# Weight halves made during the second layers and kept in DRAM, constants and bias behind the first inputs, and the first output column group freed before the exponent

## The reference

```
for e in (real, imaginary):                        # first and second layers
    h_e = gelu(layernorm(x @ W1_e.T + b1_e) * g_e + be_e)   # x: 1024 x 2048, W1: 2048 x 2048
    s_e = (h_e @ W2_e.T + b2_e)                             # W2: 2048 x 2048, cut into 4 states of 512
q, k, v for e: s_e @ Wq_e.T + bq_e, ...                     # six 512 x 512 matrices, 8 heads
mag = sqrt(|q . conj(k)|^2 + 1e-8) / 8;  w = softmax(mag)   # over the 4 states
attn_e = (w @ v_e) @ Wo_e.T + bo_e                          # two 512 x 512 matrices
R, I = attn turned by int_Wr[n], int_Wi[n]                  # per state n, eight 512 x 512 matrices
f = cos(phase between states i and j) * strength
sup = normalised sum over i, j of f * (R, I)
amp = |meas (Mr, Mi) applied to sup|;  z = gelu(layernorm(amp @ post_W.T + b))
y = relu(relu([z, x] @ W_top1 + b) @ W_top2 + b) @ W_top3
```

## Time and profile before

| what | us |
|---|---|
| median of 3 runs | 3175.93 |
| lowest, highest | 3175.32, 3177.78 |
| time of the profiled execution | 3182.69 |
| its span | 3181.0 |
| PE busy in it | 2999.9 |
| DVE busy | 1573.5 |
| ACT busy | 1111.3 |

### The profile page before, as it was taken

One profiled execution on the slowest core, in us unless ns is written; L12 is line 12 of the kernel. 1 busy time (PEld: TensorE's weight loads), 2 busy tenths in 40 slices (PEclk: granted clock), 3 DMA queues, 4 the chain that ended last, 5 costly groups with the idle time before them and its releaser, 6 DMA issues. The chain is left out here.

```text
span 3181.0 us, 43948 instructions
## 1 busy us (share of the span) xinstructions
PE 2999.9 (94%) x15808; PEld 2577.4 (81%) x15808; DVE 1573.5 (49%) x2819; ACT 1111.3 (35%) x1873; POOL 232.9 (7%) x241
## 2 busy tenths in 40 slices
PE   7999999999699999999969999999999989999798
PEld 6888888888588877888859999999999977777686
DVE  3222222112531125212156766767757768999973
ACT  3111111111331114211145555555545564555553
POOL 1000000000110011111000000000000000112000
PEclk9999999999899999999989999999999999999899
DMA  5222222121442334332252232232232274444410
GB/s 196 73 76 73 73 75 73 57 65 63 149 143 75 99 96 136 106 99 84 71 185 54 56 90 66 66 86 59 66 92 53 80 189 89 99 88 96 142 41 11
DMA packets 364352, 285.48 MB, mean 90 GB/s; under 512 B 280192, under 2 KB 280320, under 8 KB 364160
## 3 DMA queue, kind: packets, MB, share of 16 engines
q1 hardware_dynamic: 341632, 206.97, 24.3%
q0 software_dynamic: 22656, 77.67, 7.1%
HBM read 194.40 MB, written 90.18 MB: 89 GB/s over the span
## 5 line engine op out<-in xcount | busy, mean ns | idle before, releaser
L50 PE MATMUL banks<-a_whi,a_xhi 128*128 128x512 f32 x1152 | 450.4, 391 | 24.1 <-DVE a_wlo L179 17.6
L51 PE MATMUL banks<-a_wlo,a_xhi 128*128 128x512 f32 x1152 | 449.4, 390 | 0.0
L52 PE MATMUL banks<-a_whi,a_xlo 128*128 128x512 f32 x1152 | 449.3, 390 | 0.0
L50 PE MATMUL banks<-b_ghi,b_whi 128*128 128x512 f32 x1024 | 402.1, 393 | 10.2 <-DVE b_slo L389 8.6
L52 PE MATMUL banks<-b_ghi,b_wlo 128*128 128x512 f32 x1024 | 399.1, 390 | 0.0
L51 PE MATMUL banks<-b_glo,b_whi 128*128 128x512 f32 x1024 | 399.0, 390 | 0.0
L179 DVE TENSOR_TENSOR a_wlo<-a_wraw,a_whi 128x512 fp32r<-128x512 f32 x144 | 99.7, 693 | 577.6 <-ACT a_whi L165 577.6
L165 ACT ACTIVATE a_whi<-a_wraw 128x512 fp32r<-128x512 f32 x144 | 90.9, 631 | 668.1 <-PE banks L52 629.3
L50 PE MATMUL banks<-t_sx,s_whi 128*128 128x256 f32 x1024 | 292.8, 286 | 28.6 <-DVE s_wlo L1267 24.5
L374 DVE TENSOR_TENSOR b_wlo<-b_wraw,b_whi 128x512 fp32r<-128x512 f32 x128 | 88.3, 691 | 444.8 <-ACT b_whi L326 444.6
L52 PE MATMUL banks<-t_sx,s_wlo 128*128 128x256 f32 x1024 | 289.9, 283 | 0.0
(11 more groups left out here) (156 smaller groups left out, 5562.9 us busy)
## 6 DMA issues: line engine op xcount, KB each, us to landing
a_wraw<-w_first SPq DMA_DIRECT2D x144, 256.0 KB, 2.6
b_wraw<-w_second SPq DMA_DIRECT2D x128, 256.0 KB, 2.6
t_sx<-s_scr SPq DMA_DIRECT2D x64, 512.0 KB, 4.5
a_scr<-t_at SPq DMA_DIRECT2D x256, 128.0 KB, 2.1
s_axng<-a_scr SPq DMA_DIRECT2D x64, 512.0 KB, 5.6
s_wraw<-w_pieces SPq DMA_DIRECT2D x82, 256.0 KB, 4.7
h_scr<-a_hst POOLq DMA_DIRECT2D x72, 256.0 KB, 2.7
b_hl<-h_scr POOLq DMA_DIRECT2D x16, 1024.0 KB, 6.0
```

What stands on the lines that cost most here:

```text
L50: mm(out, ahi, bhi, start=first, stop=False)
L51: mm(out, ahi, blo, start=False, stop=False)
L52: return mm(out, alo, bhi, start=False, stop=last)
```

## The change

1. `phase_constants` is gone. POOL makes the constants in the first stage after its 16 loads of the input; SP loads the first nine weight tiles, then the columns and the bias, then goes on.
2. Halves of the late weights are made in the second layers. In chunks 1 to 6 of both branches, 6 pieces each (`PRE`), 4 in the last chunk of the first branch, 6 in the first of the second: SP loads a piece (256 KB), ACT and DVE split it (`pre_high`, `pre_low`, after the ring's own steps j = 3 to 7, by `AFTER`), SP stores both halves (512 KB) to the new `w_scr` in DRAM.
3. `g.hi` and `g.lo` (32 tiles each) now lie where `xhi`/`xlo`, `ghi`/`glo` and `whi`/`wlo` of the stages lay. `load_pieces(q, group)` loads four pieces, high and low, with two transfers of 1 MB. As steps q = 0 to 7 of the last second-layer chunk end, the first 8 groups are loaded over `ghi`, `glo`. The rest follows in the states stage, in place of `piece` on SP. PE waits for the loads (`g.w_in[q]`), and all `pieces` are gone from ACT and DVE.
4. In `block_body`, group 0 of `t_high` and `t_low` comes before `exponent` and `total`.

```diff
@@ first layers @@
+            def load_w(c, k):
+                sp.wait_ge(w_split, c * KI + (k + 1))
+                sp.dma_start(wraw[:, k % RAW, :], g.w_first[c, k]).then_inc(w_loaded[k % RAW], 16)
+            for k in range(KI):
+                load_w(0, k)
+                if k == KI // 2:
+                    sp.dma_start(g.cols[:, :], g.cols_in).then_inc(cols_in, 16)
+                    sp.dma_start(bias[:, :], g.row1.rearrange("c n -> (c n)").partition_broadcast(P)).then_inc(bias_in, 16)
...
@@ second layers @@
+        praw = s.sb("praw", [P, 2, W])
+        pnew = s.sb("pnew", [P, 2, 2, W], F32R)
...
+        AFTER = {3: (0, 1), 4: (2,), 5: (3,), 6: (4,), 7: (5,)}
...
+            def pre_load(p, x):
+                sp.wait_ge(p_split, p + 1)
+                sp.dma_start(praw[:, x % 2, :], g.w_pieces[p]).then_inc(p_loaded[x % 2], 16)
+            def pre_store(p, x):
+                sp.wait_ge(p_split, p + 3)
+                sp.dma_start(g.w_scr[bass.ds(p, 1)].rearrange("o p h w -> p (o h) w"),
+                             pnew[:, x % 2, :, :].bitcast(F32)).then_inc(p_stored[x % 2], 16)
+            def chunk(br, c, n):
                 for j in range(ST):
+                    ring(br * CH + c, j)
+                    if j < min(n, 2):
+                        pre_load(prepared(br, c, j), j)
+                    for x in AFTER.get(j - 1, ()) + ((5,) if j == ST - 1 else ()):
+                        if x < n:
+                            pre_store(prepared(br, c, x), x)
+                        if x + 2 < n:
+                            pre_load(prepared(br, c, x + 2), x + 2)
...
+            for q in range(ST):
+                sp.wait_ge(w_used, (2 * CH - 1) * ST + (SPL + q + 1))
+                g.load_pieces(sp, q, q)
...
+            def pre_high(p, x):
+                act.wait_ge(p_loaded[x % 2], (p - x) * 8 + (16 * (x // 2) + 16))
+                act.wait_ge(p_stored[x % 2], (p - x) * 8 + (16 * (x // 2) + 16))
+                act.activation(pnew[:, x % 2, 0, :], praw[:, x % 2, :], ACT.Copy).then_inc(p_hi, 1)
...
@@ states, SP @@
             sp.wait_ge(projected, LAST_B * 8 + 8)
-            for i in range(NP, NP + 2 * KD):
-                piece(i)
+            for q in range(4):
+                g.load_pieces(sp, q, 8 + q)
             sp.wait_ge(v_full, LAST_B * 4 + 4)
             load(0, 0)
+            for q in range(4, 6):
+                g.load_pieces(sp, q, 8 + q)
             store_a(LAST_B - 1)
             load(0, 1)
-            for i in range(NP + 2 * KD, NP + 4 * KD):
-                piece(i)
             store_a(LAST_B)
...
+            for q in range(6, 8):
+                g.load_pieces(sp, q, 8 + q)
             load(0, 2)
...
+            sp.wait_ge(multiplied, LAST * 8 + 2)
+            g.load_pieces(sp, 0, 16)
+            g.load_pieces(sp, 1, 17)
             load(LAST, 3)
             store(LAST - 2)
+            sp.wait_ge(multiplied, LAST * 8 + 4)
+            g.load_pieces(sp, 2, 18)
+            g.load_pieces(sp, 3, 19)
             sp.wait_ge(multiplied, LAST * 8 + 6)
             sup_back(0)
...
@@ states, ACT (DVE alike, with t_low before total) @@
                 t_magnitude(b)
+                if not first and not last(b):
+                    t_high(b - 1, 0)
                 exponent(b)
                 if not first and not last(b):
-                    for m in range(KD):
+                    for m in range(1, KD):
                         t_high(b - 1, m)
...
@@ build @@
+        def load_pieces(eng, q, group):
+            n = min(KD, NPIECE - group * KD)
+            for h, to in enumerate((g.hi, g.lo)):
+                eng.dma_start(to[:, q * KD:q * KD + n, :].bitcast(F32),
+                              g.w_scr[group * KD:group * KD + n, :, h, :].rearrange("i p w -> p i w")).then_inc(g.w_in[q], 16)
```

More of the change, by code:

```diff
@@ L423, in _ @@
                                           ALU.subtract).then_inc(g_split, 1)
+                    for x in AFTER.get(j, ()):
+                        if x < extra(br, 0):
+                            pre_low(prepared(br, 0, x), x)
                 for j in range(AHEAD):
@@ L429, in _ @@
                         w_low(br * CH + c, j)
+                        for x in AFTER[j]:
+                            pre_low(prepared(br, c, x), x)
                     for j in range(AHEAD):
@@ L436, in _ @@
                     w_low(br * CH + (CH - 1), j)
+                    for x in AFTER[j]:
+                        if x < extra(br, CH - 1):
+                            pre_low(prepared(br, CH - 1, x), x)
                 s_low(br, CH - 1)
@@ L514, in phase_states @@
     with s.ctx:
[L515 to L519 removed]
+        whi, wlo = g.hi, g.lo
         ids = s.sb("ids", [P, TT, N], mybir.dt.int32)
@@ L830, in _ @@
             sup_back(2)
-            for i in range(2 * NP + 4 * KD, 2 * NP + N_TOP):
-                piece(i)
             store(LAST - 1)
@@ L950, in block_body @@
                         o_high(b - 1, m - 1)
-                    if first and m == 1:
-                        pieces(M_V * KD, M_O * KD)
-                    if first and m == 3:
-                        pieces(M_O * KD, NP)
                 if not first:
@@ L1286, in block_body @@
                 shift(b)
+                if not first and not last(b):
+                    t_low(b - 1, 0)
                 total(b)
@@ L1289, in block_body @@
                 if not first and not last(b):
-                    for m in range(KD):
+                    for m in range(1, KD):
                         t_low(b - 1, m)
-            pieces(0, M_V * KD)
             blocks(dve, block_body)
@@ L1513, in _ @@
             tile.units()
-            pieces(2 * NP, 2 * NP + 2 * KD)
             sup_low(0)
@@ L1712, in vectors @@
                             w = (2 * n + (x if part == 0 else 1 - x)) * KD + k
-                            if part == 0 and first:
-                                pe.wait_ge(w_split, NP + w + 1)
+                            if part == 0 and first and k == 0:
+                                pe.wait_ge(g.w_in[2 * n + x], 64)
                             a = ax[:, n % 2, :, k, :]
```

187 lines of the change are left out of this document (80 added, 107 removed).

## The result

The changed kernel takes **3192.84 us** (median of 5 runs, 3190.35 to 3197.01) against 3175.93 us before (3175.15 to 3180.23, 5 runs): a ratio of 1.0051, 95% interval 1.0037 to 1.0065. It is slower, by 16.9 us, where 3150 (3132 to 3170) was predicted: 43 us off. The profiled execution has a span of 3195.3 us, 14.3 more than before.

The account below looks back on a forecast made before the run. PE was taken as the bound nearly everywhere, DVE in the tile loop; terms -8.9 - 6.0 - 14.6 + 13.0 - 1.4 - 8.2 = -26.1 gave 3156.6 us for the profiled execution, 3149.8 by the median, taken as 3150, range 3132 to 3170.

Parts of the forecast that it names:

- the reserve that it gave SP's ring: Second layers: ring loads go out about two steps later, still one or two steps (5.4 us each) before ACT needs them.
- Second layers: Piece splits, 3.7 us per chunk on ACT and DVE each, are covered by PE's matmuls: 0, at worst +3.
- Into the first block: Between second layers and first block, loaded halves replace piece splits, so PE starts at 1615, not 1621.05: -6.0 us.
- Blocks: In fourteen blocks, group 0 ahead of exponent and total ends PE's waits of 1.045 us on average: -14.6 us.
- the margin of 0.2 to 0.3 us: In the blocks, t_low of group 1 ends 0.2 to 0.3 us before PE wants its bank; missing it gives -7.
- End of the blocks: Last block: SP's loads delay the a_scr store, ACT's group 2 comes 16.1 us later, less 3.1 behind it: +13.0 us.
- The first rival: End of the blocks: stores are not held up, giving -3.1 instead of +13.0, so 3134 us; chance 0.13.
- First tile: In the first tile, PE's wait for a negation behind pieces on ACT goes: -1.4 us.
- Pipeline: DVE splits ahead of the first measuring operand (-4.8) and of the first amplitude and its successor (-3.3) go: -8.2 us.
- Start: Until the first matmul: POOL loads x earlier (-3.8) and it lands faster without the bias (-5.2): -8.9 us.
- The second rival: Wait back at blocks' group 3 (+7.6) or chunks losing time behind SP's stores (+13); about 3165, up to 3173; chance 0.2.
- the third: load_pieces moves fewer GB/s than plain pieces, delaying the first block and end of blocks; at 250 GB/s, 3197 us; chance 0.08.

Follow-up runs that it names:

- e1: The changed kernel with 64 bytes per partition allocated ahead of hi and 64 behind lo, so both begin at a multiple of 128: 3163.46 us, ratio 0.9957.
- e2: The kernel before with the first layers' xhi and xlo moved by 64 bytes and all behind them by 128: 3185.7 us, ratio 1.0026.
- e5: The kernel before with the first layers' stationary tiles at sixteen byte offsets, one per step, weights staying at multiples of 128: 3192.97 us (one run).
- e6: The kernel before with 64 bytes allocated ahead of xhi, moving stationary and moving tiles of the first layers together: 3180.07 us (one run).
- e11: The changed kernel with 192 bytes allocated ahead of hi and 64 behind lo, and POOL instead of SP moving the second layers' pieces: 3149.9 us, ratio 0.9911.
- e4: The kernel before with only output group 0 of t_high and t_low put ahead of exponent and total: 3160.42 us, ratio 0.9938.
- e8: e1 with SP's order in the last block changed, 7.3 MB instead of 13.6 MB ahead of the first store: 3160.33 us, ratio 0.9948.
- e7: e1 with the second layers' pieces loaded and stored by POOL instead of SP: 3160.41 us, ratio 0.9945.

## Why the prediction was wrong

Its premise failed, in the first paragraph: "a change that touches no matmul can only win PE's idle time". The change touches no matmul, and it moved an operand of 6528 of them in the first two stages. The pace of PE was taken as fixed, and that is the step that failed: 22.8 + 6.8 = 29.6 us have no term in the sum. The second step that failed is the reserve that it gave SP's ring.

- **First layers: no term; +22.8 us.** The prediction has no line on the new places of `xhi` and `xlo`. e1, e2, e5 and e6 show the cause: the stationary tile lies 64 bytes off the moving one, modulo 256.
- **Second layers: 0, at worst +3; +18.1** (the stretch's 14.7 and the 3.4 won at its end). 6.8 us are the same effect, and 6.1 more stand in the first chunk of the second branch. The prediction named that place and the mechanism (SP "in order behind stores that wait for `pre_low`"), and then gave the ring two steps of reserve. It had none there: ACT waited 6.08 and 5.20 us. The worst case, +3, had no row behind it. A further 3.6 us are lost in the next chunk, where the 5.40 us of idle time were followed by the lower clock, and 1.5 in the first chunk of all, whose first step also ran at a lower granted clock (0.81 over 862.3 to 871.1); what lowered it there, no run took apart. e11, with the places right and SP's ring alone, takes 779.5 us for the whole stretch (before: 782.7) and has none of this.
- **Into the first block: -6.0; -3.4** (24.39 to 20.94). `load_pieces` had the rate assumed. What was late next were the states, as said, and later than said: SP's first load of them, behind the barrier, is at 1646.14, some 15 us after the last second-layer matmul (before: some 9), with the DMA engines full until then.
- **Blocks: -14.6; -17.2 by e4.** The mechanism is right, and the margin of 0.2 to 0.3 us held. A wait of 1.05 us ended, and 1.3 us per block was won; the sum took the row's idle time for the whole. Why it is more, no run shows.
- **End of the blocks: +13.0; +9.0 for the stall, +1.3 behind it.** ACT's group came 42.8 us after the first load's issue (2539.03 to 2581.80), where it was 28.4: +14.4 for the +16.1 of the sum. What follows to PE's turn was 10.63 us and is 3.52: 7.1 shorter, where 3.1 was taken off. PE itself was 1.7 us earlier relative to that first load, so that its wait grew by 9.0. e8 confirms the queue. The first rival (stores not held up) falls with it.
- **First tile: -1.4; nothing.** 1.37 for a negation became 1.81 for a landing of `s_axng`.
- **Pipeline: -8.2; -8.6**, though by another path: measuring waits 7.72 instead of the forecast 5.5. And the pipeline that the change does not touch took 189.5 us in the kernel before but 186.6 in e2 to e5, so that the gain is 5.7 to 8.6.
- **Start: -8.9; -6.7.** Input at 7.91 us, not 5.7: the load landed in 6.5 us, above the 4.7 taken and just outside the bound of 6.0.

With the misplaced tiles put right and SP's ring freed, the change gives 3149.9 us (e11), where 3150 was said. That agreement is luck. In e11's profile the start gives -7.1, the second layers and the way into the first block -3.2 (said: -6.0), the blocks and their end -11.8 (said: -1.6), the loop -2.3 and the pipeline -8.2: together 33 us under the profile before, not 26. The 7 us between are what the forecast took off for a slow profiled execution before. Part of the blocks' gain is place again: they last 57.5 us each in e1 and e11, 57.7 in the changed kernel and in e4. The second rival (a cover thinner than thought) was right in kind, and gave 3165 to 3173, though its own prices, +7.6 and +13, add up to 3170 at most; the third (slow loads) named the right side for a reason that the windows refute.

## What to carry to other kernels

A change of what is allocated first is a change of every matmul whose operands move: compare the places of stationary and moving tiles modulo 256 before and after, and count matmuls in equal windows, since PE is shown busy either way. A queue that feeds the bound engine should hold nothing that waits for another engine's result; put the new transfers on a queue with idle time. Order loads and stores on one queue by when they are needed, since a store waits for what stands ahead of it: 13.6 MB took 42.8 us here from the first load's issue until ACT could go on. How much of that is felt depends on when the store is needed: 10.5 MB more ahead of it than before let ACT go on 14.4 us later. And look behind a stall that the change brings: 5.40 us without a matmul were followed by several us at the lower clock.

## What the runs showed of the hardware

- Float32 matmuls of 128 x 512 with a weight load each, start to start: 226.7 ns where stationary and moving tile begin at the same place modulo 256 bytes, 228.9 at 192, 231.7 at 128, 233.3 at 64 and most others. A common shift of 64 bytes does not matter (e6). One chunk of the changed kernel ran at 233.3 where the rule gives 228.9. Why is open: no run shows more than the pace. For 256 columns the aligned form was no faster (119.9 against 118.4 ns).
- Stores of 256-byte runs from a tile 128 bytes off a multiple of 256 took 8.2 us to land instead of 5.1, and with them PE's wait for the hidden layer was 6.67 us (e7) instead of 0.42 (e11).
- 13.6 MB of loads ahead in a queue held a 128 KB store for 13 us after its issue (2568.76 to 2581.80), though such a store lands in 2.1 us as a median.
- After 5.40 us without a matmul the granted clock fell to its lower level (1.2 GHz), and the matmuls came every 427 ns until 5.7 us after PE's restart, instead of every 229.
